# Macaron layer on one Trainium2 core: expert slots interleaved in pairs, one-hot rows compared in half precision

## The reference, cut to what matters

```python
# x: (8, 256, 128), E = 8 experts, 2 experts per token, capacity 40 slots per expert and sequence
probs = softmax(x @ Wr)
topk_probs, topk_experts = top_k(probs, 2)
pos = (how many earlier (token, choice) entries of this sequence chose the same expert)
keep = pos < capacity
buf[e_flat, b_idx, pos_c] += x_rep * keep                 # tokens into slots
h = relu(einsum('ebnc,ech->ebnh', buf, W1) + b1)
y = einsum('ebnh,ehc->ebnc', h, W2) + b2
y_tok = y[e_flat, b_idx, pos_c] * keep * p_flat           # slots back to tokens
out = y_tok.reshape(B, T, K, C).sum(axis=2)
...
x = x + 0.5 * ffn(layernorm(x))
x = x + attention(layernorm(x))
x = x + 0.5 * ffn(layernorm(x))
```

## Time and profile before

| | |
|---|---|
| median of 3 runs | 198.16 us |
| lowest to highest | 197.95 to 198.96 us |
| the profiled execution's own time | 198.15 us |
| its span in the profile | 196.4 us |
| PE busy | 182.0 us (93%) |
| ACT busy | 153.6 us (78%) |
| DVE busy | 142.9 us (73%) |
| POOL busy | 68.2 us (35%) |
| one-hot operations (line 783) | 16, 15.2 us together |

### The profile page before, as it was taken

How to read it: one execution, slowest core, us unless ns; L and a number is a source line. 1 busy time by engine, 2 the same in 40 slices (tenths; PEclk the granted TensorE clock), 3 DMA queues, 4 the chain that set the end, 5 groups by cost and what they waited for, 6 DMA issues and landing times.

```text
span 196.4 us, 6048 instructions
## 1 busy us (share of the span) xinstructions
PE 182.0 (93%) x2329; PEld 145.4 (74%) x2329; DVE 142.9 (73%) x408; ACT 153.6 (78%) x361; POOL 68.2 (35%) x104
## 2 busy tenths in 40 slices
PE   7918799999999999999999999999999999999962
PEld 7905599999988966754646656655699998999952
DVE  0899977889989588879337958889986665345572
ACT  3785698939976859999899998998798977786430
POOL 8975632000050006665765576789000000000000
PEclk9996999999999999999999999999999999999999
DMA  4999100000005599558766746700000000000213
GB/s 129 324 324 333 49 0 5 0 3 0 3 0 166 147 224 262 153 131 204 229 191 172 220 133 167 198 5 0 3 3 0 3 0 0 3 2 3 62 50 107
DMA packets 21742, 19.69 MB, mean 100 GB/s; under 512 B 1705, under 2 KB 18641, under 8 KB 21713
## 3 DMA queue, kind: packets, MB, share of 16 engines
q1 hardware_dynamic: 21568, 19.29, 36.1%
q10 hardware_dynamic: 144, 0.00, 0.0%
HBM read 14.05 MB, written 5.24 MB: 98 GB/s over the span
## 4 chain that ended last, share of the span: by engine, by line
PE 77%; DVE 14%; ACT 3%; issue 2%; POOL 2%; DVEq 0%; ACTq 0%; POOLq 0%
PE psB L993 19%; PE psB L1063 7%; PE psS L1046 4%; PE psS L870 4%; PE psS L871 4%; PE psS L872 4%; PE psB L880 4%; PE psB L969 3%; PE psB L1065 3%; PE psB L951 3%; PE psB L929 3%; DVE xn L711 2%; DVE oh L783 2%; PE psB L1002 2%; PE psB L1084 2%
## 5 line engine op out<-in xcount | busy, mean ns | idle before, releaser
L550 POOL TENSOR_SCALAR_AFFINE_SELECT amat<-amat 128x512 f32<-128x512 f32 x64 | 44.4, 702 | 36.7 <-ACT amat L631 35.3
L631 ACT ACTIVATE amat<-psS 128x768 f32<-128x768 f32 x64 | 48.9, 813 | 3.7 <-PE psS L1048 3.2
L602 ACT ACTIVATE hid<-psS,biasT 128x160 f32<-128x160 f32 x128 | 39.4, 405 | 6.0 <-PE psS L872 5.5
L993 PE MATMUL psB<-hid,w 128*128 128x160 f32 x256 | 40.4, 304 | 0.1
L993 PEld LDWEIGHTS psB<-hid,w 128*128 128x128 f32 x256 | 35.6, 190 | 0.7 <-issue 0.4
L870 PE MATMUL psS<-xe,w 128*128 128x160 f16 x128 | 27.2, 232 | 1.1 <-ACT biasT L582 0.9
L872 PE MATMUL psS<-xe,w 128*128 128x160 f16 x128 | 27.2, 233 | 0.0
L871 PE MATMUL psS<-xe,w 128*128 128x160 f16 x128 | 27.2, 233 | 0.0
L1063 PE MATMUL psB<-amat,vst 128*32 128x256 f32 x256 | 20.4, 389 | 0.2 <-POOL amat L550 0.2
L610 ACT ACTIVATE yT<-psB,biasT 128x160 f32<-128x160 f32 x32 | 12.2, 408 | 7.0 <-PE psB L993 7.0
L711 DVE TENSOR_SCALAR xn<-x,meanvar,rstd 128x128 f32<-128x128 f32 x40 | 15.9, 459 | 0.4
(11 more groups left out here) (155 smaller groups left out, 374.2 us busy)
## 6 DMA issues: line engine op xcount, KB each, us to landing
qk_parts<-qk SPq DMA_DIRECT2D x16, 256.0 KB, 3.5
stack<-qk_parts SPq DMA_DIRECT2D x16, 256.0 KB, 3.8
stack<-qk_parts SPq DMA_DIRECT2D x32, 128.0 KB, 3.9
amat<-in_L_ffn_W SPq DMA_DIRECT2D x8, 256.0 KB, 5.3
w<-in_L_ffn_W SPq DMA_DIRECT2D x8, 256.0 KB, 5.5
x<-in_L_attn_hidden_states SPq DMA_DIRECT2D x4, 256.0 KB, 4.8
out<-x SPq DMA_DIRECT2D x8, 128.0 KB, 1.9
amat<-in_L_attn_Wq SPq DMA_DIRECT2D x1, 128.0 KB, 4.2
```

What stands on the lines that cost most here:

```text
L550: pool.affine_select(out=d, in_=d, pattern=[[0, 2], [0, 2], [1, P]], compare_op=ALU.is_ge, fill=0.0, base=0, channel_multiplier=-1).then_i ...
L602: ins = act.activation(hid[:, n % 2, c, :], psS[:, wide_slot(s) + c // 2, (c % 2) * GS:(c % 2 + 1) * GS], ACT.Relu, bias=biasT[:, e * HC + ...
L631: act.activation(amat[:, n % A_RING, :, :], psS[:, wide_slot(s):wide_slot(s) + 2, 0:T + P], ACT.Square)\
L993: ins = mm(bank(s)[:, 0:GS], w2[:, e, c, :], hid[:, n % 2, c, :], start=(c == 0), stop=(c == HC - 1))
```

## The change

The slots of two experts are interleaved. Slot number was 40 e + c; it is now 80 h + 2 c + l for expert e = 2 h + l. The code follows this in six places. The one-hot comparison has `key` in float16 and an `iota` that holds every number twice, so that all three operands have neighbouring elements side by side, and is issued per tile of 128 tokens instead of per sequence: 8 operations of 320 elements per unit instead of 4 of 640. The copy to `xe` reads PSUM with a step of two elements, and ACT writes `yT` with a step of two. `pmask` is no longer made by POOL; POOL makes a smaller `psel` of 12 elements, DVE sums `ident` to a parity per partition at its start, and multiplies and copies the two to `pmask` at its first `pw`. The wait of `yt` names expert 3, 7 and 7 instead of 3, 6 and 7. The scratch of `iota` moves from `cand` to `ldiff`.

```diff
-        key = sb("key", [P, TT, GB, E])
+        key = sb("key", [P, TT, GB, E], f16)
...
-        iota = sb("iota", [P, CAP], f16)
+        iota = sb("iota", [P, CAP, 2], f16)
...
-                move(eng, xe[:, parity(l, g), int(kind == "dpl"), :, i * CAP:(i + 1) * CAP],
-                     bank(s)[:, 0:SLOTS].rearrange("p (e c) -> p e c", e=E)).then_inc(taken(s), 1)
+                move(eng, xe[:, parity(l, g), int(kind == "dpl"), :, i * CAP:(i + 1) * CAP].rearrange("p (h l) c -> p h l c", l=2),
+                     bank(s)[:, 0:SLOTS].rearrange("p (h c l) -> p h l c", h=EP, l=2)).then_inc(taken(s), 1)
...
-            pool.iota(iota_i, pattern=[[1, CAP]], base=1, channel_multiplier=0)
+            pool.iota(iota_i, pattern=[[1, CAP], [0, 2]], base=1, channel_multiplier=0)
...
-                    act.activation(yT[:, parity(l, g), :, e * CAP:(e + 1) * CAP],
+                    act.activation(yT[:, parity(l, g), :, 0:SLOTS].rearrange("p b (h c l) -> p b h c l", h=EP, l=2)[:, :, e // 2, :, e % 2],
...
+            def make_pmask():
+
+                dve.wait_ge(consts_made, 2)
+                link(dve.tensor_tensor(pslots[:, :, :, :].rearrange("p k h l -> p (k h) l"),
+                                       psel[:, :, :].rearrange("p k h -> p (k h)").unsqueeze(2).broadcast_to([P, KT * EP, 2]),
+                                       parity_of[:, :].unsqueeze(1).broadcast_to([P, KT * EP, 2]), ALU.mult))
+                for b in range(GB):
+                    n = KT * 2 * E
+                    ins = dve.tensor_copy(pmask[:, b * n:(b + 1) * n].rearrange("p (k a e) -> p k a e", k=KT, a=2),
+                                          pslots[:, :, :, :].rearrange("p k h l -> p k (h l)").unsqueeze(2).broadcast_to([P, KT, 2, E]))
+                link(ins)
+
             dve.wait_ge(consts_made, 1)
+            link(dve.tensor_reduce(parity_of[:, :], ident[:, :].rearrange("p (j l) -> p l j", l=2), AX.X, ALU.add))
...
                     for i in range(GB):
-                        dve.tensor_tensor(
-                            oh[:, parity(*s[1:]), TT * i:TT * i + TT, 0:SLOTS].rearrange("p a (e c) -> p a e c", e=E),
-                            iota[:, :].unsqueeze(1).unsqueeze(1).broadcast_to([P, TT, E, CAP]),
-                            key[:, :, i, :].unsqueeze(3).broadcast_to([P, TT, E, CAP]),
-                            ALU.is_equal).then_inc(oh_ready, 1)
+                        for a in range(TT):
+                            ins = dve.tensor_tensor(
+                                oh[:, parity(*s[1:]), TT * i + a, 0:SLOTS].rearrange("p (h c l) -> p h c l", h=EP, l=2),
+                                iota[:, :, :].unsqueeze(1).broadcast_to([P, EP, CAP, 2]),
+                                key[:, a, i, :].rearrange("p (h l) -> p h l", l=2).unsqueeze(2).broadcast_to([P, EP, CAP, 2]),
+                                ALU.is_equal)
+                        ins.then_inc(oh_ready, 1)
                 elif kind == "pw":
                     _, l, g = s
                     if n == 0:
-                        dve.wait_ge(consts_made, 2)
+                        make_pmask()
...
-                    pe.wait_ge(y_taken, nth[("down", l, g, min(((k + 1) * P - 1) // CAP, E - 1))] + 1)
+                    pe.wait_ge(y_taken, nth[("down", l, g, min(2 * (((k + 1) * P - 1) // (2 * CAP)) + 1, E - 1))] + 1)
```

More of the change, by code:

```diff
@@ L45 @@
 KT = 3
+EP = E // 2
 SP_ = KT * P
@@ L240, in macaron_program @@
         pmask = sb("pmask", [P, GB * KT * 2 * E])
+        psel = sb("psel", [P, KT, EP])
+        parity_of = sb("parity_of", [P, 2])
+        pslots = sb("pslots", [P, KT, EP, 2])
         pslot = sb("pslot", [P, 2, GB * KT])
@@ L270, in macaron_program @@
         upper16 = sb("upper16", [P, P], f16)
-        iota = sb("iota", [P, CAP], f16)
+        iota = sb("iota", [P, CAP, 2], f16)
         rank = sb("rank", [P, E])
-        iota_i = cand[:, :, :].rearrange("p t e -> p (t e)")[:, 0:CAP].bitcast(i32)
+        iota_i = ldiff[:, :, :, :].rearrange("p u t e -> p (u t e)")[:, 0:2 * CAP].bitcast(i32)
         rank_i = rest[:, 0, :].bitcast(i32)
@@ L509, in _ @@
                                fill=0.0, base=0, channel_multiplier=-1)
-            pool.tensor_copy(iota[:, :], iota_i)
+            pool.tensor_copy(iota[:, :, :].rearrange("p c l -> p (c l)"), iota_i)
             pool.tensor_copy(rank[:, :], rank_i).then_inc(consts_made, 1)
             pool.memset(oh[:, :, :, SLOTS:], 0.0)
-            pm = pmask[:, :].rearrange("p (b k a e) -> p b k a e", b=GB, k=KT, a=2)
-            link(pool.memset(pmask[:, :], 1.0))
-            link(pool.affine_select(out=pm, in_=pm, pattern=[[0, GB], [P, KT], [0, 2], [-CAP, E]],
+            link(pool.memset(psel[:, :, :], 1.0))
+            link(pool.affine_select(out=psel[:, :, :], in_=psel[:, :, :], pattern=[[P, KT], [-2 * CAP, EP]],
                                     compare_op=ALU.is_ge, fill=0.0, base=0, channel_multiplier=1))
-            last = pool.affine_select(out=pm, in_=pm, pattern=[[0, GB], [-P, KT], [0, 2], [CAP, E]],
-                                      compare_op=ALU.is_gt, fill=0.0, base=CAP, channel_multiplier=-1)
+            last = pool.affine_select(out=psel[:, :, :], in_=psel[:, :, :], pattern=[[-P, KT], [2 * CAP, EP]],
+                                      compare_op=ALU.is_gt, fill=0.0, base=2 * CAP, channel_multiplier=-1)
             last.then_inc(consts_made, 1)
```

## The result

The changed kernel is slower. Its median is 200.25 us (8 runs, 199.33 to 201.17), beside 198.78 for the kernel before on the same chip (8 runs, 197.95 to 199.28). The ratio is 1.0088 with an interval of 1.0065 to 1.0111. As a difference the ratio is 0.0088 x 198.78 = 1.75 us, where the forecast had 0.45. The eight times fall into two groups, four at 199.3 to 199.7 and four at 200.8 to 201.2. The profiled execution, 201.17 us with a span of 199.4, belongs to the upper group.

What follows compares the result with a forecast made beforehand. PE was taken as the bound, with 77% of the chain of waits, so DVE counts only where PE, or ACT ahead of it, waits. 198.15 - 0.4 + 0.6 - 0.2 + 0.5 = 198.65, say 198.6 us; range 197.3 to 199.9.

Steps and rivals of the forecast that it cites:

- term 4: Last transposes, unit (1,1): PE waits for ACT's write of expert 7 before the second `yt` tile; +0.5 us (+0.4 to +0.6).
- The price of a comparison: One-hot comparisons on DVE: 320 elements take about 0.33 us alone and 0.25 apart, 0.41 apart at full price.
- Term 1: First unit: first sequence ready 0.73 us later, last comparison 0.93 earlier, second `down` 0.35 to 0.4 earlier; -0.4 us.
- a rival with a chance of 0.07: Start: PE begins 0.7 us later after idling, so its clock comes back later; 199.5 us, chance 0.07.
- The port rival: First unit: DVE keeps the port for both halves, first sequence ready at 15.2; 198.25 or 197.5 us, chance 0.2.
- Term 2: First masked product: five mask operations on DVE delay the first `cb` on PE; +0.6 us (+0.3 to +1.1).
- Unit (0,1): Comparisons end 0.9 us earlier but DVE then waits for PE, and ACT's write ends during another transpose; zero.
- Term 3: Unit (1,0): short comparisons hold POOL's masking less, so PE's 0.22 us wait goes; -0.2 us (0 to -0.6).
- Term 5: Copy to `xe`, reading PSUM at every second float: stepped access costs zero.
- the rival in which ACT pays for the step: Six copies before the first `up`: stepped elements cost ACT twice, 1.6 us more; 200.2 us, chance 0.08.
- full price* rival: Comparisons get no speed per element: start +0.4, mask +0.6, unit (1,0) 0, end +0.5; 199.65 us, chance 0.1.
- the slack case: Slack elsewhere eats the losses of mask or end while the start keeps its gain; 197.5 us, chance 0.08.

Runs made afterwards that it cites:

- runs 8: The kernel before with only `key` in float16, its elements still repeated 40 times; one execution, 199.16 us.
- run 9: The changed kernel with `key` back in float32, pair order and two operations per tile kept; 201.87 us, ratio 1.0203.
- run 2: The changed kernel with padding matmuls on PE, 6 behind the last `down` and 20 ahead of the last `ca`; 199.38 us, ratio 1.0058.
- Run 6: The changed kernel with POOL waiting for all first-unit comparisons ahead of its first subtraction instead of its third; 199.08 us, ratio 1.0040.
- run 4: The kernel before with five DVE operations of the mask's sizes added ahead of its first masked product, into scratch tiles; 198.57 us, ratio 1.0025.
- Run 1: The kernel before with one edit: its second weighted transposes wait for expert 7 instead of 6; 200.80 us, ratio 1.0095.

## Why the prediction was wrong

The step that failed is term 4, the end. All terms, in order:

- **The price of a comparison**: right. 0.318 us alone and 0.236 apart, for 0.33 and 0.25. The Trainium skill (VectorE: DVE Perf Modes, sections Mode 2×_1P and The perf-mode tier table) has two elements per cycle for a two-input operation with all operands 16-bit and step one; runs 8 and 9 agree with it, each lacking one of the two conditions (0.82 us for 640 elements, 0.484 for 320).
- **Term 1, the start, -0.4**: the steps were right, the end was wrong. The first gather came 0.70 later, counted from the first comparison (forecast 0.73), the last comparison 1.05 earlier (0.93), the second `hid` 0.35 earlier (0.35 to 0.4). But the second `down` came only 0.11 earlier. I let it follow ACT. PE's own row is the reason: from the first `up` at 22.54 it has work without a gap to 26.62, 4.08 us, and the first `up` was late by the late first sequence. Before, the same stretch took 4.89 us (21.39 to 26.28), so it held 0.81 of slack. The first `up` came 0.70 later, and 0.11 is what was left. The prediction named PE's own work as a limit only for the case that the first sequence isn't late; it was the limit in the other case. In run 2 the start is even 0.44 us longer than before: there the clock came back later, which the prediction had as a rival with a chance of 0.07. The port rival is out: the second half of the first sequence did wait for POOL. Run 6 shows the gain that lay behind it all, 1.0 us.
- **Term 2, the mask, +0.6**: the size was right, +0.48 in the trace and +0.5 in run 4; the path was not. The prediction let PE wait in front of its first `cb`, and named a first `cb` without a wait as a sign that it is wrong. There is none: PE stands earlier, at the slot transposes at 43.05, for the bank of the masked product, and works without a gap from there.
- **Unit (0,1), 0**: +0.16. The trace has the same longer wait there as at the end: ACT's `yT` at 70.43 stands in the chain ahead of the transposes at 70.98. The prediction said that ACT's write ends in time.
- **Term 3, unit (1,0), -0.2**: the mechanism was right, -0.45 measured, within its ends of 0 and -0.6. The product that had waited for POOL starts 3.42 us after the first comparison instead of 3.73, so 0.31 of it is there, where the term counted the wait of 0.22; the rest comes behind it.
- **Term 4, the last transposes, +0.5**: this is the step that failed. Its own size was 0.78: the term counted 0.44 us of standing and a step, but not that the four transposes behind it take 0.64 in the chain instead of 0.45. Far more, the sum stopped at the weighting and took all that follows as unchanged. PE's waits behind it grew from 1.41 us to 0.58 and 1.74, and the granted clock fell ahead of the last combine, for another 1.6 us. Run 1 shows both with this wait alone, run 2 that the clock stays up when the idle time is filled. The prediction had a rival on the clock, but put it at the start, where the profile had shown a low clock.
- **Term 5, stepped access, 0**: right. ACT's 24 copies into `xe` have a median of 0.437 us, 0.438 before; the rival in which ACT pays for the step is out.

With the terms as measured, counted in the profiled execution, the sum is -0.11 + 0.48 + 0.16 - 0.45 + 0.78 = 0.86 without the clock at the end; run 2 measures 1.2, with its longer start, and the lower group of the changed kernel's times lies 0.8 above the median before. The clock adds 1.63 in the executions in which it falls. If these are the four of eight in the upper group, the mean is 0.86 + 0.5 x 1.63 = 1.68 us, against 1.75 by the ratio. The *full price* rival, given 199.65, is measured by run 9 at 201.87: its start was priced, its stay in POOL's way in unit (1,0), set at 0, was not.

The chances hold two slips. 0.1 + 0.08 + 0.07 + 0.04 is 0.29, not 0.28. And half of the port case and a part of the slack case are counted as below 197.2, though the lowest time worked out for either is 197.5.

## What to carry to other kernels

Where a wait in front of the last dependent work grows, price what comes behind it at both clocks: here 0.9 us more of idle time made 3.4 us of path into 5.0 in some of the executions, and 26 padding matmuls in the two gaps kept the clock up. Splitting an operation on an engine that takes turns with another makes the first complete result later, unless the other is held away; then the shorter operations pay. And a gain on one path is worth no more than the slack of the next one, so check the next engine's own gapless work from the same point.

## What the runs showed of the hardware that was not expected

- PE's granted clock at the end fell in three of five profiles with the same waits (0.58 and 1.74 us with eight transposes between) and stayed up in two. It did not fall in the profiles with a single idle time of 1.4 us, or with 0.25 and 0.62 and padding matmuls. Which of the two longer idle times decides, or the whole 3.37 us in which PE only transposes, no run tells apart.
- Two profiles with the same start differ in when the clock is low there. It falls to 0.50 while PE stands ahead of the first gather, and is low from 13.4 to 20.2 us in the changed kernel's profile, from 15.0 to 21.8 in that of run 2, where the second `down` comes 0.55 us later.
- A comparison of 320 elements takes 0.318 us with all in half precision and equal neighbours adjacent, 0.484 with one operand in full precision; at 640 elements with each key repeated over 40 slots 0.82, whether the key is in half precision or not.
- Beside POOL's masking the short comparisons are slowed too: eight take 3.74 us instead of 1.97, while POOL's seven take 4.97 us, and 6.17 beside four long comparisons.
